# A graph attention network on one core: every engine's instructions in a new order

## What is computed

```python
def gat(inp, adj, W, a):
    h = inp @ W
    f1, f2 = h @ a[:F, 0], h @ a[F:, 0]
    e = leaky_relu(f1[:, :, None] + f2[:, None, :], 0.2)
    if adj is not None:
        e = where(adj > 0, e, -9e15)
    return elu(softmax(e, axis=2) @ h)

h = relu(layernorm(x))
o1 = relu(h @ mlp1_w + mlp1_b)                  # 256 features
z = elu(gat(o1, None, W_fc, a_fc)) + o1         # layer 1, no mask
o2 = relu(z @ mlp2_w + mlp2_b)                  # 128 features
x = x + relu(elu(gat(o2, adj, W_hand, a_hand)) + o2)   # layer 2
h = relu(layernorm(x))
x = x + gat(h, adj, W, a)                       # layer 3
```

## Time and profile before

| what | before |
| --- | --- |
| median of 3 runs | 432.83 us |
| profiled execution, span | 429.0 us |
| PE busy | 411.1 us (96%) |
| DVE busy | 357.8 us (83%) |
| ACT busy | 315.7 us (74%) |
| share of PE in the chain that ended last | 87% |
| bytes moved by DMA | 36.42 MB, mean 85 GB/s |

### The profile page before, as it was taken

One profiled execution on the slowest core, in us unless ns is written; L12 is line 12 of the kernel. 1 busy time (PEld: TensorE's weight loads), 2 busy tenths in 40 slices (PEclk: granted clock), 3 DMA queues, 4 the chain that ended last, 5 costly groups with the idle time before them and its releaser, 6 DMA issues.

```text
span 429.0 us, 8704 instructions
## 1 busy us (share of the span) xinstructions
PE 411.1 (96%) x2544; PEld 352.7 (82%) x2544; DVE 357.8 (83%) x1226; ACT 315.7 (74%) x764; POOL 24.9 (6%) x53
## 2 busy tenths in 40 slices
PE   6999999999999999999999999999999999989782
PEld 4688779887898899797998788989879799869772
DVE  7786588878998898988898868979698899889974
ACT  2655659658796787786878688687867887799774
POOL 0000000000001000010100000100000000000000
PEclk9999999999999999999999999999999999999997
DMA  7854323123423142232222213222320122120001
GB/s 209 278 146 130 105 74 121 74 76 98 125 98 75 53 138 84 52 101 74 75 82 68 75 53 98 79 72 74 80 87 10 49 93 59 45 80 24 27 1 57
DMA packets 39461, 36.42 MB, mean 85 GB/s; under 512 B 4080, under 2 KB 30320, under 8 KB 39408
## 3 DMA queue, kind: packets, MB, share of 16 engines
q1 hardware_dynamic: 37408, 33.17, 26.1%
q10 hardware_dynamic: 2000, 2.63, 1.8%
HBM read 31.46 MB, written 4.32 MB: 83 GB/s over the span
## 4 chain that ended last, share of the span: by engine, by line
PE 87%; DVE 5%; ACT 3%; issue 2%; DMA 1%; SPq 0%; POOL 0%; ACTq 0%; DVEq 0%
PE bank L1530 24%; PE bank L1437 23%; PE bank L1426 13%; PE bank L1416 6%; PE bank L1477 6%; PE bank L1455 6%; PE bank L1445 3%; PE bank L1538 2%; PE bank L1496 1%; PE bank L1466 1%; DMA row<-row_scratch 1%; DVE stats L1036 1%; DVE u L1265 1%; ACT ext L826 1%; ACT e L911 1%
## 5 line engine op out<-in xcount | busy, mean ns | idle before, releaser
L1530 PEld LDWEIGHTS bank<-ext,prob 128*128 128x128 f32 x1024 | 119.6, 192 | 6.3 <-issue 4.9
L1530 PE MATMUL bank<-ext,prob 128*128 128x129 f32 x1024 | 122.1, 275 | 0.3 <-DVE prob L1207 0.2
L1437 PE MATMUL bank<-ext,prob 128*128 128x257 f32 x512 | 119.0, 380 | 0.0
L1437 PEld LDWEIGHTS bank<-ext,prob 128*128 128x128 f32 x512 | 94.8, 190 | 17.3 <-issue 4.5
L1211 DVE SCALAR_TENSOR_TENSOR prob<-prob,square,mask_t 128x512 f32<-128x512 f32 x98 | 70.6, 739 | 0.9 <-ACT prob L859 0.8
L1426 PE MATMUL bank<-wfc_sb,o_t 128*128 128x259 f32 x256 | 64.0, 382 | 0.4 <-ACT o_t L790 0.4
L859 ACT ACTIVATE prob<-row,square 128x512 f32<-128x512 f32 x78 | 54.1, 720 | 0.1
L1426 PEld LDWEIGHTS bank<-wfc_sb,o_t 128*128 128x128 f32 x256 | 46.3, 190 | 9.6 <-issue 4.5
L903 ACT ACTIVATE y<-bank,recip 128x128 f32<-128x128 f32 x128 | 39.3, 369 | 15.3 <-DVE recip L1257 14.2
L911 ACT ACTIVATE e<-y,minus_one 128x512 f32<-128x512 f32 (+1 forms) x70 | 47.7, 688 | 1.4
L1265 DVE SCALAR_TENSOR_TENSOR u<-e,y 128x512 f32<-128x512 f32 (+1 forms) x70 | 44.1, 638 | 4.2 <-issue 2.2
(11 more groups left out here) (98 smaller groups left out, 499.1 us busy)
## 6 DMA issues: line engine op xcount, KB each, us to landing
row<-row_scratch SPq DMA_DIRECT2D x36, 256.0 KB, 3.3
...
x_in<-in_x SPq DMA_DIRECT2D x16, 256.0 KB, 5.3
x_res<-in_x SPq DMA_DIRECT2D x16, 256.0 KB, 4.6
out<-y_out SPq DMA_DIRECT2D x15, 256.0 KB, 3.9
normed<-in_x_t SPq DMA_DIRECT2D x14, 256.0 KB, 4.3
...
```

Of the source, the lines that this page charges most:

```text
L1437: last = nc.tensor.matmul(filled[:, 0:H + 1], gat1.targets(b, t, c), gat1.features_and_one(b, t), start=(t == 0), stop=(t == C - 1))
L1530: last = nc.tensor.matmul(filled[:, e * (D + 3):e * (D + 3) + D + 1], L.targets(b, t, c), L.features_and_one(b, t), start=(t == 0), stop=( ...
```

## The change

Only the strings of `ORDER` change; no step is added or removed, and each list has the same words as before (SP 113, GpSimd 49, ACT 582, DVE 685, PE 388). A word moves by 2.5 places in the mean on SP, 3.5 on ACT, 4.0 on DVE, 1.8 on PE and 0.4 on GpSimd. Since the table became nine lines shorter, a line number of the changed kernel is 9 less than that of the same line before. Two lines of the difference:

```diff
     "sync": """
-        load.0 load.1 load_t.0 weights load.2 load_again.0 load.3 load.4 load_t.3 weights_rest load.5 load.6
+        load.0 load_t.0 weights load.1 load.2 load_again.1 load.3 load.4 weights_rest load_t.3 load.5 load.6 load.8
```

More of the change, by code:

```diff
@@ L70 @@
[L70 to L109, removed]
@@ L115 @@
[L115 to L118, removed]
+        weights root1.0 root1.1 adjacency turn1.1 root1.2 mlp1_0.0 mlp1_1.0 mlp1_0.1 mlp1_1.1 h1_0.0 h1_1.0 h1_2.0
@@ new lines @@
+        att1_3.2 prob2_1.1 elu1_1.2 prob2_2.1 att2_0.0 att2_1.0 elu2.0 prob2_3.1 att1_0.3 att1_1.3 att1_2.3 att1_3.3
+        elu1_0.3 elu1_1.3 turn2.0 args1.4 mlp1_0.5 mlp1_1.5 att2_0.1 att2_1.1 elu2.1 h1_0.5 root2.0 root1.9 mlp2.2
+        h3_0.0 h2_0.2 root1.10 h1_1.5 h1_2.5 h1_3.5 h3_1.0 h2_1.2 args1.5 att1_0.4 args3.0 root2.1 row3.0 args2.2
+        turn2.1 att1_1.4 att1_2.4 mlp2.3 att1_3.4 elu1_0.4 prob3_1.0 h3_0.1 h3_1.1 h2_0.3 h2_1.3 mlp1_0.6 prob2_1.2
+        mlp1_1.6 elu1_1.4 att1_0.5 prob3_2.0 att1_1.5 prob3_3.0 args3.1 prob2_2.2 args2.3 prob2_3.2 att1_2.5 h1_0.6
@@ new lines @@
+        prob3_2.2 prob3_3.2 turn2.3 h1_0.8 h1_1.8 att1_2.6 h3_0.3 h3_1.3 att1_3.6 root1.14 elu1_0.6 elu1_1.6
+        att2_0.5 att2_1.5 att3_0.2 h1_2.8 att3_1.2 args3.3 h1_3.8 elu2.5 elu3.2 args1.8 mlp2.6 h2_0.6 h2_1.6
+        mlp1_0.9 prob3_1.3 att1_0.7 att1_1.7 prob3_2.3 prob3_3.3 mlp1_1.9 att1_2.7 att1_3.7 turn2.4 root2.4 elu1_0.7
+        elu1_1.7 h1_0.9 h1_1.9 h3_0.4 att3_0.3 args2.6 att3_1.3 elu3.3 h1_2.9 h1_3.9 h3_1.4 args3.4 args1.9
+        mlp1_0.10 mlp1_1.10 root2.5 att1_0.8 prob2_1.6 prob2_2.6 turn2.5 prob2_3.6 att1_1.8 att1_2.8 prob3_1.4
@@ new lines @@
+        prob2_3.6 prob3_0.4 prob3_1.4 prob3_2.4 max3.5 args3.5 att2_0.6 att2_1.6 prob3_3.4 normt.11 normt.12
+        stats1.15 row3.5 max2.7 prob1_0.9 prob1_1.9 elu2.6 norm1.14 max1.10 prob1_2.9 elu1_0.8 prob1_3.9 args2.7
+        elu1_1.8 att3_0.4 att3_1.4 args1.10 row2.7 z_0.8 prob3_0.5 att1_0.9 prob3_1.5 prob3_2.5 prob3_3.5 elu3.4
+        att1_1.9 att1_2.9 result.4 x1.6 z_1.8 norm2.6 row1.10 att3_0.5 att3_1.5 prob2_0.7 root2n.6 att1_3.9
+        prob2_1.7 prob2_2.7 prob2_3.7 elu1_0.9 elu1_1.9 prob1_0.10 prob1_1.10 elu3.5 prob1_2.10 prob1_3.10 max3.6
@@ L217 @@
-        att2_1.15 turn2.14 h3_0.14 h3_1.14 row3.14 turn2.15 h3_0.15 h3_1.15 att3_0.14 row3.15 att3_1.14
-        att3_0.15 att3_1.15
+        warm means.0 roots.0 scores1 mlp1_0.0 turn1.1 mlp1_1.0 mlp1_0.1 mlp1_1.1 h1_0.0 h1_1.0 h1_2.0 h1_3.0 h1_0.1
+        h1_1.1 h1_2.1 turn1.2 scores23 row1.0 h1_3.1 empties mlp1_0.2 att1_0.0 att1_1.0 att1_2.0 row1.1 mlp1_1.2
+        att1_3.0 h1_0.2 h1_1.2 h1_2.2 h1_3.2 att1_0.1 att1_1.1 att1_2.1 att1_3.1 z_0.0 z_1.0 mlp1_0.3 mlp1_1.3
+        mlp2.0 h1_0.3 h1_1.3 h1_2.3 h1_3.3 row1.2 z_0.1 z_1.1 h2_0.0 h2_1.0 mlp1_0.4 mlp1_1.4 mlp2.1 att1_0.2 row2.0
```

247 lines of the change are left out of this document (132 added, 115 removed).

## The result

The changed kernel takes 445.5 us (median of 4 runs, 443.9 to 447.1), beside 432.8 us (431.7 to 433.1) for the kernel before on the same chip: a ratio of 1.031, 95% interval [1.027, 1.034]. The forecast was 436.2 us with a range of 433.6 to 438.2. The direction was right and the size was not: the change costs about 13 us, and the forecast had 3.4. Lines of the changed kernel are those of before less 9.

The account below looks back on a forecast made before the run. PE was taken as the bound, with a matmul always in flight from 12.16 to 379 us. Span 429.0 + 3.2 (start) + 0.2 (middle) + 0 (tail) = 432.4 us, plus 3.8 to the median: 436.2 us, range 433.6 to 438.2.

Parts of the forecast that it names:

- x of batch 1: At the start, load.1 as SP's fourth transfer lands at 7.7 us (5.3 to 8.2), and stats1.1 on DVE waits for it.
- first rival: At the start, x of batch 1 lands by 5.3 us: 433.5 us, no measurable change; chance 0.15.
- second rival: The tail gives back more than the start costs; with 5 us won there, 431.2 us; chance 0.07.
- The start: Up to h1_0.0: costs 2.85 us with the full clock, about 3.7 with the half; taken as 3.2 us.
- full clock: PE at 2.4 GHz at the start: mlp1_0.0 at about 12.0 us, h1_0.0 at 16.75, a cost of 2.85 us.
- half-rate case: PE restarts at 1.2 GHz after its pause: mlp1_0.0 at 13.1 us, the start costing about 3.7 us.
- third rival: Half rate lasts beyond h1_0.0 (1.5 us of matmuls), or the middle stalls; with both, 439 us; chance 0.16.
- The middle: PE's full stretch between start and tail: 0.2 us lost, with 0 and 1.5 us as ends.
- The attention's inputs have as much room as before or more: In the middle, PE time between a step and its user is no shorter for these inputs.
- The tail: The end of the kernel, where PE waits for z_0.15: 0 us together, between -0.4 and +0.5.
- The sum: Whole kernel: 429.0 + 3.2 + 0.2 + 0 = 432.4 us of span, 436.2 us as median.
- step from span to median: Whole kernel: the median lies 3.8 us above the span shown, so 432.4 us of span becomes 436.2 us.

Follow-up runs that it names:

- stir_gap: The changed kernel with 16 instead of 2 identity transposes on PE ahead of the second group of roots.0: 441.8 us, ratio 1.021.
- new_start: Every engine's list has the changed kernel's order up to 19 us, then that of the kernel before: 436.6 us, ratio 1.010.
- norm_first: The changed kernel with stats1.1 moved behind vectors and norm1.0 in DVE's list: 443.5 us, ratio 1.026.
- old_start: Every engine's list has the order of the kernel before up to 15 us, then the changed kernel's: 440.8 us, ratio 1.020.
- queue_order: old_start with six attention rows moved ahead of other batches' statistics rows or prefetches in SP's list: 435.4 us, ratio 1.006.

## Why the forecast was right and wrong

**x of batch 1: right, with too low an upper bound.** The load, issued at 2.3 us, landed at 8.07 where 7.7 was taken (bounds 5.3 and 8.2). In the three other kernels with the same first loads it landed at 8.4 (stir_gap), 8.6 (new_start) and 8.9 us (norm_first). From the DMA issues of the changed kernel, KB and us to landing, as in the earlier trace rows:

```profile
x_in<-in_x SPq DMA_DIRECT2D x1, 256.0 KB, 5.8
w_sb<-in_L_gnn_mlp_w SPq DMA_DIRECT2D x1, 128.0 KB, 3.9
```

The Trainium skill (DMA: Bandwidth & Descriptors, Anatomy of one DMA) would have 2.6 us for it, as an estimate; the trace, with 5.8 us, does not agree. The first rival, x by 5.3 us, falls. (The forecast gave the total by that rule as the second rival's; an early x is its first rival, 433.5 us.)

**The start: the right mechanism, too small.** The sum had 3.2 us. new_start alone measures 4.2, the profile 4.9. The 4.9 are against the profile of before, which is of a quick execution: its `h1_0.0` came at 12.16 us, and over the eight profiles with that start the mean is 12.7, against which the start costs 4.3 us. With the full clock the step's times were nearly exact: stir_gap has `mlp1_0.0` at 11.9 (12.0 forecast), `turn1.1` at 13.35 (13.4) and `h1_0.0` at 16.57 (16.75). The mis-sized term is the half rate. `mlp1_0.0` started at 13.09 as the half-rate case said. But that case charged the half rate only up to there: `mlp1_0.0` itself then took 1.71 us where it takes 0.86, so that `turn1.1` started at 14.80 and not 14.3, and the products of `mlp1_1.0`, to 16.7 us, ran at half rate too. From 13.09 us on PE has no wait, so each of these adds in full, and `h1_0.0` came at 18.76 instead of 17.6. That was the third rival's clock half (its "1.5 us of them"), and it belonged in the sum, since PE's pause was already in it. What spoke against it, that PE works without pause from about 10 us, was true (from 9.94 us) and didn't bring the full rate before 16.7.

**The middle: the step that failed.** "The attention's inputs have as much room as before or more", and so 0.2 us for the middle, with 1.5 as the upper end. It measures 8.6 us (old_start). I had counted room in PE's time between a step and the one that needs its result. The row has a path of its own, from DVE through SP to memory, back through SP to all partitions, and on to ACT and DVE, and it never touches PE. Nothing in its length changed (5.5 us before, 5.6 now, medians of the rows for which SP was free); what changed was how close ACT's and DVE's use stands behind it, and what SP is doing at the moment. In the order of before, the first use of a row comes 2.2 us behind its landing (median of the 36 rows that go by SP), and four rows are used within 0.35 us of landing, so that their user was or may have been waiting. In the new order the median is 0.03 us, and there are 23. Two rows waited over 1 us for SP to begin their write before; now there are five, the worst 6.1 us, four of them in line behind another row step that holds SP until its write has landed. By queue_order, the places in SP's list are 5.8 of the 8.6 us; the rest, the short distance itself, was not taken apart. The forecast named SP's queue only at the start and in the tail.

**The tail: right.** PE's longest wait there, before `z_0.15`, is 1.67 us behind the `u` of ACT's two exponentials (row below), as long as before, and the idle time after 364 us is 0.2 us less than before. The second rival (a tail that gives back 5 us) falls.

```profile
395.58 1.09 PE L1436 MATMUL bank<-ident,u 128*128 128x128 f32 x8 [1.67 <-DVE u L1256]
```

**The sum.** 4.2 for the start, 8.6 for the middle and about 0 for the tail are 12.8 us, against 13.2 measured. The forecast's step from span to median, 3.8 us, was right for the kernel before and too much for the profile of the changed one: every execution on record lies 1.7 to 1.9 us above its span, and the other 2 us were that the profile of before was of a quick one.
